# Expert routing by pairs of tiles, and the first eight expert blocks of a group fixed, in a six-layer decoder kernel

## The reference

```python
x = x + _L0_attn_ref(_layernorm(x, axis=-1), ...)            # causal attention, quantised weights and inputs
x = x + _L0_xattn_ref(ctx, ctx, _layernorm(x, axis=-1), ...) # attention over the context
x = x + _L0_ffn_ref(_layernorm(x, axis=-1), ...)             # mixture of 8 experts, 2 per token
x = x + _L1_attn_ref(_layernorm(x, axis=-1), ...)            # linear attention
x = x + _L1_xattn_ref(_layernorm(x, axis=-1), ctx)           # most similar row of the context
x = x + _L1_ffn_ref(_layernorm(x, axis=-1), ...)             # fixed-point feed-forward
```

```python
logits = x @ gate_w                                   # 8 per token
mult, sel = _sparse_mixer_routing(logits)             # top 2 and their weights
h = silu(einsum('th,ehf->etf', x, w1)) * einsum('th,ehf->etf', x, w3)
out = einsum('etf,efh,te->th', h, w2, w)              # w is 0 but for the two chosen
```

## Time and profile before

| | us |
|---|---|
| three runs | 353.76, 354.57, 356.07 |
| median | 354.57 |
| profiled execution, its own time | 352.06 |
| its span, first to last instruction | 350.3 |
| busy: TensorE, VectorE, ScalarE, GpSimd | 288.3, 236.8, 187.0, 143.8 |

### The profile page before, as it was taken

How to read it: one execution, slowest core, us unless ns; L and a number is a source line. 1 busy time by engine, 2 the same in 40 slices (tenths; PEclk the granted TensorE clock), 3 DMA queues, 4 the chain that set the end, 5 groups by cost and what they waited for, 6 DMA issues and landing times.

```text
span 350.3 us, 11308 instructions
## 1 busy us (share of the span) xinstructions
PE 288.3 (82%) x4176; PEld 225.1 (64%) x4176; DVE 236.8 (68%) x796; ACT 187.0 (53%) x531; POOL 143.8 (41%) x179
## 2 busy tenths in 40 slices
PE   1858999999998879999895879999986487997464
PEld 1324676667666569999784868999975256864243
DVE  3887688988868765426835137734676999676784
ACT  1599834457432416455442347774538297634571
POOL 8199041326403725235684377513551832012000
PEclk9978999999999989999999899999999579999768
DMA  8940000000000537647884686446630100000001
GB/s 266 402 184 1 10 5 3 2 4 5 3 2 12 174 113 248 222 145 255 263 249 124 220 276 200 157 153 205 209 123 16 38 24 17 18 6 0 0 0 32
DMA packets 19767, 38.41 MB, mean 110 GB/s; under 512 B 2152, under 2 KB 13032, under 8 KB 19584
## 3 DMA queue, kind: packets, MB, share of 16 engines
q1 hardware_dynamic: 17504, 34.59, 29.8%
q0 software_dynamic: 1024, 2.10, 2.0%
q10 hardware_dynamic: 1184, 1.00, 0.9%
HBM read 29.88 MB, written 7.73 MB: 107 GB/s over the span
## 4 chain that ended last, share of the span: by engine, by line
PE 54%; DVE 12%; issue 11%; DMA 9%; ACT 9%; POOL 4%; POOLq 0%; SPq 0%; ACTq 0%; DVEq 0%
PE FU L555 11%; PE OA L564 5%; PE OA L741 5%; PE FU L682 4%; PE Sp L667 3%; DMA xg<-xall,slot 3%; DMA keyT<-yg,home 3%; ACT keyT L981 2%; PE Sp L682 2%; DMA text<-in_ctx 2%; PE OA L770 2%; PE Mp L858 2%; POOL xg L482 2%; PE OA L781 1%; PE Mp L710 1%
## 5 line engine op out<-in xcount | busy, mean ns | idle before, releaser
L555 PE MATMUL FU<-xgT,wbuf 128*128 128x128 f32 x480 | 65.1, 284 | 4.5 <-DVE hh L1446 3.2
L460 POOL TENSOR_TENSOR hh<-hh,uu 128x256 f32<-128x256 f32 x60 | 43.1, 733 | 59.3 <-DVE hh L1446 59.0
L555 PEld LDWEIGHTS FU<-xgT,wbuf 128*128 128x128 f32 x480 | 59.6, 197 | 6.5 <-DMA wbuf<-in_w 3.7
L454 POOL TENSOR_TENSOR rstd<-powed,minus_half 128x1 f32<-128x1 f32 (+1 forms) x36 | 22.0, 612 | 75.5 <-DVE powed L1122 61.9
L1446 DVE SCALAR_TENSOR_TENSOR hh<-th,FU 128x256 f32<-128x256 f32 x60 | 24.7, 420 | 41.3 <-ACT uu L886 40.9
L454 POOL TENSOR_TENSOR rms<-rms,minus_half 128x20 f32<-128x20 f32 x8 | 29.2, 3649 | 24.3 <-DVE rms L1216 24.3
L896 ACT ACTIVATE th<-FU 128x256 f32<-128x256 f32 x60 | 23.2, 387 | 23.8 <-PE FU L555 23.3
L564 PE MATMUL OA<-wbuf,hh 128*128 128x128 f32 x240 | 33.6, 284 | 1.8 <-ACT ys L886 1.3
L564 PEld LDWEIGHTS OA<-wbuf,hh 128*128 128x128 f32 x240 | 30.1, 197 | 3.1 <-ACT ys L886 1.5
L886 ACT ACTIVATE uu<-FU 128x256 f32<-128x256 f32 x60 | 23.3, 389 | 0.0
L973 ACT ACTIVATE keys<-Qp,params,consts 128x128 f32<-128x128 f32 x64 | 23.2, 483 | 0.0
(11 more groups left out here) (264 smaller groups left out, 678.1 us busy)
## 6 DMA issues: line engine op xcount, KB each, us to landing
wbuf<-in_w SPq DMA_DIRECT2D x30, 768.0 KB, 4.6
xg<-zeros SPq DMA_DIRECT2D x2, 2048.0 KB, 15.7
xg<-xg SPq DMA_DIRECT2D x30, 64.0 KB, 3.1
yg<-ys SPq DMA_DIRECT2D x30, 64.0 KB, 2.9
params<-in_params SPq DMA_DIRECT2D x1, 1503.5 KB, 10.2
x<-in_x ACTq DMA_DIRECT2D x1, 512.0 KB, 4.6
text<-in_ctx SPq DMA_DIRECT2D x1, 512.0 KB, 7.1
out<-x SPq DMA_DIRECT2D x4, 128.0 KB, 1.8
```

The source lines that it names most:

```text
L454: return nc.gpsimd.tensor_tensor(o, base, exponent[:, 0:o.shape[1]], ALU.pow)
L460: nc.gpsimd.tensor_tensor(hh[:, u % NB, :], hh[:, u % NB, :], uu[:, u % NB, :], ALU.mult)\
L555: ins = mm(FU[:, v % 2, 256 * part + P * i:256 * part + P * i + P], wbuf[:, u % WB, c:c + P], xgT[:, u % 2, :], start=True, stop=True)
```

## The change

The eight first blocks of a group are now fixed: block j is the first 128 rows of expert j's region, whose address is known when the kernel is built. `W:u` of such a block waits only for its buffer, and `X:u` for its buffer and the scatters. Only blocks 9 to 15 of a group come from the table, which has 7 rows now, and counts blocks beyond an expert's first. `spread` gives tokens beyond an expert's first 128 rows another place, which takes five instructions more. `route`, `rank` and `slots` take a pair of tiles q instead of a group, and `scat` waits for its own pair's slots. All five order tables are new. Of their lines only a few are shown here, and the old bodies of `rank`, `route` and `slots`, are left out.

```diff
+LAST = [(FIRST[g] + SIZE[g]) // 2 - 1 for g in range(NGRP)]
...
-        scat:4 scat:5 scat:6 scat:7 rstd:14 rstd:15 bias:12 bias:13 bias:14 bias:15 h:0 h:1 prstd:2 h:2 h:3 h:4 h:5 h:6 h:7
...
+        scat:4 scat:5 rstd:13 scat:6 scat:7 rstd:14 rstd:15 bias:13 h:0 h:1 h:2 h:3 h:4 bias:14 h:5 prstd:2 bias:15 h:6 h:7
...
-        X:11 X:12 X:13 W:10 W:11 W:12 X:14 W:13 Y:6 Y:7 W:14 W:15 Y:8 Y:9 Y:10 Y:11 X:15 Y:12 W:16 X:16 X:17 Y:13 Y:14 W:17
...
+        Y:4 Y:5 W:10 Y:6 W:11 X:13 X:14 W:12 W:13 Y:7 W:14 Y:8 Y:9 Y:10 Y:11 W:15 X:15 W:16 X:16 X:17 Y:12 Y:13 Y:14 W:17 X:18
...
             def weights_in(u):
                 g, j = UNIT[u]
-                sp.wait_ge(C["tab_ready"], g + 1)
                 if u >= WB:
                     sp.wait_ge(C["down_mm"], u - WB + 1)
-                row = sp.value_load(tab[g][0:1, 0, j:j + 1], min_val=0, max_val=(E - 1) * P)
+                if j < E:
+                    sp.dma_start(wbuf[:, u % WB, :], d["w"][j * P:j * P + P, :]).then_inc(w_loaded[u % WB], 16)
+                    return
+                sp.wait_ge(C["tab_ready"], g + 1)
+                row = sp.value_load(tab[g][0:1, 0, j - E:j - E + 1], min_val=0, max_val=(E - 1) * P)
                 sp.dma_start(wbuf[:, u % WB, :], d["w"][bass.ds(row, P), :]).then_inc(w_loaded[u % WB], 16)
 
             def rows_in(u):
                 g, j = UNIT[u]
-                sp.wait_ge(C["tab_ready"], g + 1)
                 sp.wait_ge(scattered[g], 16 * 2 * SIZE[g])
                 if u >= WB:
                     sp.wait_ge(C["xgT_mm"], u - WB + 1)
-                row = sp.value_load(tab[g][0:1, 1, j:j + 1], min_val=0, max_val=E * REGION - P)
+                if j < E:
+                    sp.dma_start(xg[:, u % WB, :], d["xg"][g][j * REGION:j * REGION + P, :]).then_inc(xg_loaded[u % WB], 16)
+                    return
+                sp.wait_ge(C["tab_ready"], g + 1)
+                row = sp.value_load(tab[g][0:1, 1, j - E:j - E + 1], min_val=0, max_val=E * REGION - P)
                 sp.dma_start(xg[:, u % WB, :], d["xg"][g][bass.ds(row, P), :]).then_inc(xg_loaded[u % WB], 16)
...
                 g = GROUP[t]
-                pool.wait_ge(C["slot_ready"], g + 1)
+                pool.wait_ge(C["slot_ready"], t // 2 + 1)
...
+            def rank(q):
+
+                g = GROUP[2 * q]
+                t = 2 * q - FIRST[g]
+                fill("Mp", (C["rank_took"], q + 1))
+                pe.wait_ge(C["hot_ready"], q + 1)
                 pe.wait_ge(tabs_ready, 1)
+
+                def chosen_in(i):
+                    return hot_b[g][:, i * E:i * E + E]
+
+                mm(Mp[:, 0:2 * E], before_b[:, :], hot_b[g][:, t * E:t * E + 2 * E], start=True, stop=False, skip_group_check=True)
+                for i in range(t):
+                    mm(Mp[:, 0:2 * E], ones_b[:, :], chosen_in(i).unsqueeze(1).to_broadcast([P, 2, E]), start=False, stop=False,
                        skip_group_check=True)
+                ins = mm(Mp[:, E:2 * E], ones_b[:, :], chosen_in(t), start=False, stop=True, skip_group_check=True)
+                if q == LAST[g]:
+                    for i in range(SIZE[g]):
+                        ins = mm(Mp[:, 2 * E:3 * E], ones_b[:, :], chosen_in(i), start=i == 0, stop=i == SIZE[g] - 1,
+                                 skip_group_check=True)
                 ins.then_inc(C["rank_mm"], 1)
...
+            def both(a):
+                return a.unsqueeze(1).to_broadcast([P, 2, a.shape[1], E])
...
+            def route(q):
+
+                g = GROUP[2 * q]
+                tt = slice(2 * q - FIRST[g], 2 * q - FIRST[g] + 2)
+                dve.wait_ge(C["lg_in"], q + 1)
                 if g:
+                    dve.wait_ge(C["rank_mm"], FIRST[g] // 2)
+                top(g, 0, tt)
+                link(v.scalar_tensor_tensor(base[g][:, 1, tt, :], hot[g][:, 0, tt, :], -3.0e38, base[g][:, 0, tt, :], ALU.mult, ALU.add))
+                top(g, 1, tt)
+                v.tensor_tensor(hot_b[g][:, tt.start * E:tt.stop * E].rearrange("p (t e) -> p t e", e=E), hot[g][:, 0, tt, :],
+                                hot[g][:, 1, tt, :], ALU.add).then_inc(C["hot_ready"], 1)
+
+            def slots(q):
+
+                g = GROUP[2 * q]
+                tt = slice(2 * q - FIRST[g], 2 * q - FIRST[g] + 2)
+                dve.wait_ge(C["rank_mm"], q + 1)
+                ins = v.tensor_tensor(place[g][:, tt, :], Mp[:, 0:2 * E].rearrange("p (t e) -> p t e", e=E),
+                                      ebase.unsqueeze(1).to_broadcast([P, 2, E]), ALU.add)
+                if q == LAST[g]:
+                    link(ins)
+                    ins = v.tensor_scalar(tiles_of[:, :], Mp[:, 2 * E:3 * E], 1.0, 1.0 / P, ALU.max, ALU.mult)
+                ins.then_inc(C["rank_took"], 1)
+                dve.wait_ge(C["rank_took"], q + 1)
+                link(v.tensor_tensor(chosen[g][:, :, tt, :], hot[g][:, :, tt, :], both(place[g][:, tt, :]), ALU.mult))
+                link(v.tensor_reduce(slot_f[g][:, :, tt], chosen[g][:, :, tt, :], X, ALU.add))
+                v.tensor_copy(slot[g][:, :, tt], slot_f[g][:, :, tt]).then_inc(C["slot_ready"], 1)
...
+                n = UNITS_OF[g] - E
+                dve.wait_ge(C["rank_took"], LAST[g] + 1)
+                link(v.tensor_scalar(tiles_of[:, :], tiles_of[:, :], (P - 1.0) / (2 * P) - 1.0, MAGIC, ALU.add, ALU.add))
+                link(v.tensor_scalar(tiles_of[:, :], tiles_of[:, :], MAGIC, None, ALU.subtract))
...
-                link(v.tensor_tensor(shift_of[:, :], upto[:, :], tiles_of[:, :], ALU.subtract))
-                link(v.scalar_tensor_tensor(shift_of[:, :], shift_of[:, :], float(P), ebase, ALU.mult, ALU.subtract))
-                link(v.tensor_tensor(place[g][:, :, :], place[g][:, :, :], shift_of[:, :].unsqueeze(1).to_broadcast([P, SIZE[g], E]), ALU.add))
-                link(v.tensor_tensor(chosen[g][:, :, :, :], hot[g][:, :, :, :], both(g, place[g][:, :, :]), ALU.mult))
+                each = [P, SIZE[g], E]
+                v.tensor_tensor(shift_of[:, :], upto[:, :], tiles_of[:, :], ALU.subtract)
+                v.tensor_scalar(first_of[:, :], ebase, float(P) / REGION, None, ALU.mult)
+                link(v.tensor_scalar(late[:, :], ebase, -float(P) / REGION, (E - 1.0) * P, ALU.mult, ALU.add))
+                link(v.scalar_tensor_tensor(late[:, :], shift_of[:, :], float(P), late[:, :], ALU.mult, ALU.add))
+                link(v.tensor_tensor(place[g][:, :, :], place[g][:, :, :], ebase.unsqueeze(1).to_broadcast(each), ALU.subtract))
+                link(v.scalar_tensor_tensor(beyond[g][:, :, :], place[g][:, :, :], float(P), late[:, :].unsqueeze(1).to_broadcast(each),
+                                            ALU.is_ge, ALU.mult))
+                link(v.tensor_tensor(place[g][:, :, :], place[g][:, :, :], beyond[g][:, :, :], ALU.add))
+                link(v.tensor_tensor(place[g][:, :, :], place[g][:, :, :], first_of[:, :].unsqueeze(1).to_broadcast(each), ALU.add))
+                link(v.tensor_tensor(chosen[g][:, :, :, :], hot[g][:, :, :, :], both(place[g][:, :, :]), ALU.mult))
                 link(v.tensor_reduce(slot_f[g][:, :, :], chosen[g][:, :, :, :], X, ALU.add))
                 v.tensor_copy(home[g][:, :, :], slot_f[g][:, :, :]).then_inc(C["home_ready"], 1)
```

233 lines of the change are left out of this document (102 added, 131 removed).

## The result

The changed kernel takes **341.77 us** (median of 4 runs, 340.12 to 343.87), the kernel before 355.32 beside it (4 runs). The ratio is 0.964, 95% interval 0.956 to 0.971: faster by 12.8 us, where the forecast was 349.1 (5.5 less), and outside its range (344.0 to 355.0) on the fast side. Ratios and this 12.8 leave out executions in a slow state, here one of the kernel before (361.60; the median of its other three is 354.57), and later, among others, the profiled one of base_b. The profiled execution took 341.9 us, with a span of 340.0, against 352.06 and 350.3.

A forecast was written before the change was run, and what follows sets the result against it. No engine bounds the whole kernel; TensorE holds 54% of the chain of waits. Terms -1.3 - 5.0 - 0.8 + 1.6 = -5.5 us take the profiled 352.06 to 346.6, plus 2.5 for the median: 349.1 us, range 344.0 to 355.0.

The forecast's parts named there:

- fixed blocks: First blocks' weights wait for no table; at unit 0 this removes a wait that did not end last: 0 gained.
- spreading: Longer spreading, 4.2 us, between gates 31 and 32 while TensorE is fed, 2.6 covered: 1.6 us lost (bounds 0 and 4.2).
- Pairs: First group's routing and scatters by pairs, unit 0's rows earlier: 1.3 us gained (bounds 4.5 gained, 1.1 lost).
- d: Delay of the attention chain and second pair by the first pair's routing on VectorE: 1.1 us (0 to 3.5).
- my sign of being wrong: VectorE's second logits copy coming later than 106.5 us would show the forecast wrong.
- Second group: Way into the second group of experts, third pair's scatters and stores earlier: 5.0 us gained (bounds 2.0 and 6.3).
- Combining: First gathered rows awaited two gates later, saving half of TensorE's 1.60 us wait: 0.8 gained (bounds 0 and 1.6).
- The tail: Rest of the order and the tail, root of pair 1 ahead of gathers: 0 (bounds 1.5 gained, 5.9 lost).
- The median: The kernel before's median lay 2.5 us above its profiled execution; 2.5 was added to the forecast 346.6.
- More is gained: Rival: earlier readiness counts in full at unit 0, second way in and combining; 11.3 us gained, 343.3 us; chance 0.12.
- VectorE holds attention: Rival: d is 3.5 us, and again before the last pair; 1.1 us gained in all, 353.5 us; chance 0.17.
- The hold-up by GpSimd: Rival: among the expert units GpSimd's multiplications hold short VectorE instructions, 0.45 us each; up to 358.5 us; chance 0.10.

The follow-up runs named there:

- base_b: The changed kernel, unedited, run again as the measure of the last set: 350.17 us, ratio 0.969 to the kernel before.
- run 8: The changed kernel with VectorE's spreading of group 1 ahead of gate 30 instead of behind gate 31: 340.95 us, ratio 0.959.
- run 6: The changed kernel with the last layer's root of pair 1 put back behind the fourth gather of group 1 on GpSimd: 348.37 us, ratio 0.979.
- run 9: The kernel before with the last layer's root of pair 1 moved ahead of group 1's gathers on GpSimd: 363.00 us, ratio 1.015.
- wait_late: The changed kernel with fixed weights waiting for the table and the first pair's scatters behind the second's: 348.94 us, ratio 0.988.
- stores_back: The changed kernel with the stores of units 8 to 11 behind unit 15's weights on SP: 49.4 us from half 6 to half 30.
- weights_wait: The changed kernel with fixed blocks' weights waiting for the table, first loads between the rows of units 0 to 3: 346.00 us, ratio 0.977.
- scatter_late: The changed kernel with the first pair's four scatters of group 0 behind the second pair's: 347.29 us, ratio 0.985.
- group2_late: The changed kernel with the third pair's scatters behind the fourth's: 50.4 us from half 6 to half 30, 46.7 in base_b.
- warm_late: wait_late with 18 fillers ahead of the turning of unit 0's rows: 355.43 us, ratio 0.988.
- run 11: Same as stores_back: the changed kernel, stores of units 8 to 11 behind unit 15's weights; 49.4 us from half 6 to half 30.
- run 2: Same as weights_wait: the changed kernel with fixed blocks' weights waiting for the table; 346.00 us, ratio 0.977.
- run 3: Same as scatter_late: the changed kernel with the first pair's scatters of group 0 behind the second pair's; 347.29 us, ratio 0.985.
- run 10: Same as group2_late: the changed kernel with the third pair's scatters behind the fourth's; 50.4 us from half 6 to half 30.
- run 14: The kernel before with the changed kernel's order from about half 50 to the end on all five engines: 361.08 us, ratio 1.008.
- run 15: The kernel before with the changed kernel's tail order and 22 fillers ahead of the two waits for the experts' rows: 363.54 us, ratio 1.011.
- run 16: Same as warm_late: wait_late with 18 fillers ahead of the turning of unit 0's rows; 355.43 us, ratio 0.988.

## Why the prediction was wrong

It forecast 5.5 us less and named the right places; 10.3 came in the trace and 12.8 between the medians. Three steps failed: it priced a wait at its own length, without the half clock that can follow it (2.9 to 3.1 us); it put the fixed blocks at nothing (2.0 us); and it charged 1.6 us for the spreading (0.2). A fourth error, 2.5 us, is in the median. They overlap and don't add up exactly. By its own steps:

- **Pairs 1.3 and fixed blocks 0, forecast together 1.3 for the first way in, measured 3.1 by half 6** (3.4 from the first logits copy). The last scatter went out at 115.96 as forecast (115.8). That the rows were turned at 123.03, forecast 123.0, is luck: they were there about 3 us earlier, as the scatter landed within 2.24 us and not in 4.90, and TensorE came for them only then. d was 1.96 by the bare mark (1.65 from the first logits copy) and not 1.1, so the copy came later than my sign of being wrong (106.5), and it didn't matter.
- **What the pairs' step lacks is the clock.** The step is "It gets the 2.00 us of idle time and two of the four fillers": it counts these 2.4 us, and not the 1.3 to 1.5 us of half clock behind them. It also charged d in full, although `values:13` and `out:12`, which stood ahead of the rows, had moved behind them; what that is worth no run separates.
- **Fixed blocks: forecast 0, measured 2.0 at half 0** (1.7 by the bare marks) with the pairs in place, with the medians of that set 3.4 apart, their intervals overlapping. These 2.0 are part of the 3.4, and without them the pairs alone give 1.5, near their 1.3. The step "this removes a wait that did not end last" looked at the wait only and not at the traffic. Where the pairs are in place the weights ahead of it on SP's queue slow the rows' read (6.97 against 1.68), and where the scatters are late they slow the last scatter (4.35 against 2.30).
- **Second group: forecast 5.0, measured 5.7** (half 6 to half 30). Rows at 184.93, forecast 185, is luck again: the scatter was 2.7 earlier than in the sum and the read 2.1 longer. TensorE's idle time is 2.2 of the 6.34 and not 1.3. The runs split the gain into the scatters (3.7) and the stores (2.7); they overlap. 1.6 of the 5.7 are the clock, which the step lacks, and which filled what the idle time fell short by.
- **Combining 0.8 gained, spreading 1.6 lost: forecast 0.8 lost together, measured 1.5 gained** from half 30 to half 50. TensorE's waits at the two places are the forecast 1.6 and an unchanged 1.5 (1.60 before):

```profile
194.36 1.13 PE L563 MATMUL FU<-xgT,wbuf 128*128 128x128 f32 x8 [1.64 <-DVE hh L1476]
...
202.23 0.30 PE L611 MATMUL Mp<-consts,xn 128*128 128x128 f32 x1 [1.53 <-DVE xn L1140]
```

The wait at the spreading is there as forecast, but it is no loss of its own: run 8 takes it away and gains 0.2. Nothing was gained at the combining. Where the 1.5 come from no run tells. Up to 1.0 of it may be the one execution of the kernel before (51.08), since another with the same words there took 50.05; the changed kernel took 49.46 to 50.23 in three.
- **The tail: forecast 0, measured 0** (103.36 and 103.30), as far as single executions tell: with no word of it changed, it took 103.4 and 105.3 in the old order and 103.0 to 105.8 in the new one. That it can lose is real (2.5 to 5 us in runs 6 and 9, bound 5.9), for orders that don't fit together.
- **The median: 2.5 us of the error of 7.3.** I put the kernel before's median 2.5 above its profiled execution on the new kernel too. One execution against three is no property of a kernel; the new one's differ by 0.1 and 0.6.
- **Rivals.** "More is gained" (343.3) was the nearest in number. Its mechanism, readiness counting in full, did not come: of 6.34 us of idle time on the second way 2.2 stayed, the wait at the combining stayed, at unit 0 the rows lay ready for 3 us, and the clock, which it lacks too, made up the number. "VectorE holds attention" fell: it was held 1.96 us, and the queue took it. The hold-up by GpSimd exists: VectorE's 1.85 us end at 202.09, GpSimd's 2.09 us of multiplications at 201.99. That is the one place where TensorE waits over 1 us for it. Four short instructions (at 156.60, 167.93, 170.59 and 189.37) took 0.57 to 1.28 us where their like take about 0.2, and what they cost no run tells. (The Trainium skill's page SBUF — State Buffer, section SBUF: two separate sides, has a lock for which the later of two instructions waits; the trace agrees that one waits, here until the third multiplication had ended.)

Of the 10.3 us, then, 2.9 to 3.1 are the half clock at the two waits, shown from two sides: fillers alone take it away in the kernel before, and it comes back in two of the five runs that put waits back in the changed kernel (wait_late and stores_back, not weights_wait, scatter_late or group2_late), and goes again with fillers in warm_late. Of the rest, 2.0 are the fixed blocks, and up to half 30 the others go with the idle time that the earlier rows removed, 3.3 us on the first way and 4.1 on the second, part of which the longer work on VectorE and the moved attention took back. How much they took is not shown, and the 1.5 behind half 30 are open.

## What to carry to other kernels

A wait of TensorE can cost more than its own length, namely the half clock behind it, which in this kernel was 1.3 to 2 us each time it came on the chain. The wait's length doesn't tell whether it comes (2.00 and 4.38 us had it, 2.09, 2.32 and 2.91 did not). So before pricing the removal of a wait, read the granted clock in windows of 2 us just behind it, not in one of 20, where 0.50 reads as 0.93, and in more than one execution. When two runs that each take back one part cost little, take back both: here 2.0 and 2.5 became 6.8. An edit that only takes a wait away can also free the transfers that others wait for: ask what the removed load stood beside. And one word moved in a hand-made order may cost as much as it gives when the other engines' orders belong to it, so price whole orders by marks, and set the marks where no work has changed sides.

## What was not expected of the hardware

- TensorE was granted 0.50 of its clock for some 4 us behind a wait of 2.00 us, behind 1.28 and 2.45 with a product between them, and in run 11 behind one of 1.90, but not behind 2.09 in run 2, 2.32 in run 3 and 2.91 in run 10.
- On one chip the clock was 0.50 for 8 to 24 us, and most of that time TensorE was busy (the rows are of group2_late). In four of the eight kernels (runs 9, 14, 15, 16) a stretch of 4 us in which TensorE was busy for under 2 stood just ahead of the fall, in the other four it was busy for over half of the time there. Half 0 came 4 to 10 us later there in every kernel. What sets it off no run tells.

```profile
110.00:115.00 5.00, 5.00 (x63) 3.34 (x63) 2.31 (x13) 1.55 (x4) 1.08 (x2) 0.50 0.00 0
...
120.00:125.00 5.00, 5.00 (x45) 3.25 (x48) 0.80 (x7) 1.49 (x5) 0.00 (x0) 0.50 0.20 57
```

- With two 768 KB loads ahead of it on the same queue, a 64 KB read of rows took 6.97 us and not 1.68, and behind unit 15's load 3.97 and not 1.79.
